# VectorE writes z in two 16-bit parts, DMAs turn them, and PSUM banks are dealt out anew

## The reference

```
q, k, v = einsum('bsd,dhk->bshk', x, W_Q / W_K / W_V)
scores  = einsum('bqhc,bshc->bhqs', q, k) / sqrt(64);  causal mask
z       = einsum('bhqs,bshc->bqhc', softmax(scores), v)
x = layernorm(x + einsum('bqhc,chd->bqd', z, W_out) + b_out)
h = layernorm(x) * gamma + beta
y = silu(h @ dequant(fc1_q, fc1_scales) + fc1_bias) @ dequant(fc2_q, fc2_scales) + fc2_bias
x = layernorm(x + (x + 0.5 * y))
```

## Time and profile before

| | |
|---|---|
| time, median of three | 2035.65 us (2034.11 to 2035.74) |
| the profiled execution's own time | 2037.36 us |
| its span, first to last instruction | 2035.4 us |
| TensorE busy | 1826.0 us, 90% |
| ScalarE busy | 1520.9 us, 75% |
| VectorE busy | 1418.6 us, 70% |
| GpSimd busy | 1319.7 us, 65% |
| DMA | 75.09 MB, mean 37 GB/s |

### The profile page before, as it was taken

One profiled execution on the slowest core, in us unless ns is written; L12 is line 12 of the kernel. 1 busy time (PEld: TensorE's weight loads), 2 busy tenths in 40 slices (PEclk: granted clock), 3 DMA queues, 4 the chain that ended last, 5 costly groups with the idle time before them and its releaser, 6 DMA issues. The chain is left out here.

```text
span 2035.4 us, 54700 instructions
## 1 busy us (share of the span) xinstructions
PE 1826.0 (90%) x22601; PEld 1299.9 (64%) x22601; DVE 1418.6 (70%) x2688; ACT 1520.9 (75%) x3151; POOL 1319.7 (65%) x738
## 2 busy tenths in 40 slices
PE   3788989999989898989899999999999977989997
PEld 2455756565656565656666666666666656878886
DVE  5886868676767676767767676768686838565663
ACT  3488887888888888888787878787879872654463
POOL 2365767686867686867676868686767786343242
PEclk8899999999999999999999999999999988999998
DMA  3002010101010101010101010101010205111210
GB/s 116 9 4 81 5 40 2 43 2 43 5 40 5 40 5 41 7 38 10 35 10 35 10 35 12 33 12 33 13 33 15 92 26 199 63 63 63 81 55 21
DMA packets 48647, 75.09 MB, mean 37 GB/s; under 512 B 5904, under 2 KB 32784, under 8 KB 48144
## 3 DMA queue, kind: packets, MB, share of 16 engines
q1 hardware_dynamic: 48400, 71.59, 11.2%
HBM read 33.82 MB, written 20.97 MB: 27 GB/s over the span
## 5 line engine op out<-in xcount | busy, mean ns | idle before, releaser
L459 POOL TENSOR_TENSOR p_lo<-p_full,p_hi 128x1024 f16<-128x1024 f32 (+1 forms) x640 | 1163.3, 1839 | 489.6 <-ACT p_full L507 489.2
L506 ACT ACTIVATE p_hi<-psum 128x512 f16<-128x512 f32 (+3 forms) x1280 | 721.7, 564 | 232.3 <-PE psum L774 123.0
L546 DVE TENSOR_REDUCE row_max<-psum 128x1 f32<-128x512 f32 (+3 forms) x1280 | 723.3, 604 | 98.3 <-PE psum L736 66.2
L507 ACT ACTIVATE p_full<-psum 128x512 f32<-128x512 f32 (+3 forms) x1280 | 729.1, 572 | 0.0
L794 PE MATMUL psum<-v,p_hi 128*128 128x65 f16 x4352 | 497.5, 193 | 36.3 <-DVE z_pair L591 34.1
L796 PE MATMUL psum<-v,p_hi 128*128 128x64 f16 x4352 | 499.9, 195 | 0.0
L798 PE MATMUL psum<-v,p_lo 128*128 128x65 f16 x4352 | 495.6, 192 | 0.0
L794 PEld LDWEIGHTS psum<-v,p_hi 128*128 128x128 f16 x4352 | 409.8, 96 | 102.5 <-issue 55.5
L768 PE MATMUL psum<-qa,ka 128*128 128x512 f16 (+3 forms) x1280 | 444.2, 348 | 24.6 <-ACT p_full L507 18.8
L772 PE MATMUL psum<-qb,kb 128*128 128x512 f16 (+3 forms) x1280 | 445.0, 348 | 0.0
L796 PEld LDWEIGHTS psum<-v,p_hi 128*128 128x128 f16 x4352 | 406.7, 97 | 55.4 <-issue 0.8
(11 more groups left out here) (126 smaller groups left out, 2991.9 us busy)
## 6 DMA issues: line engine op xcount, KB each, us to landing
zT_dram<-z_T SPq DMA_DIRECT2D x16, 1024.0 KB, 4.3
shared_z<-zT_dram SPq DMA_DIRECT2D x28, 512.0 KB, 6.3
qb<-qa SPq DMA_DIRECT2D x128, 64.0 KB, 1.9
ka<-ka SPq DMA_DIRECT2D x128, 64.0 KB, 1.9
shared_z<-xT_dram SPq DMA_DIRECT2D x8, 512.0 KB, 7.7
xs<-x_dram SPq DMA_DIRECT2D x8, 512.0 KB, 8.1
out_dram<-shared_w SPq DMA_DIRECT2D x8, 512.0 KB, 3.4
w_raw_rest<-wqkv_dram SPq DMA_DIRECT2D x1, 2304.0 KB, 14.6
```

Of the source, the lines that this page charges most:

```text
L459: nc.gpsimd.tensor_tensor(p_lo[:, at % NP, cols], p_full[:, at % NP, cols], p_hi[:, at % NP, cols], ALU.subtract).then_inc(probs_split, 1)
L506: nc.scalar.activation(p_hi[:, at % NP, to], lane_bank(a)[:, P * f:QB], ACT.Exp, scale=1.0 / SCORE)
L507: nc.scalar.activation(p_full[:, at % NP, to], lane_bank(a)[:, P * f:QB], ACT.Exp, scale=1.0 / SCORE).then_inc(lane_read, 1)
L546: nc.vector.reduce_max(row_max[:, n % MAXES, t, c:c + 1], bank_of(r)[:, 0:chunk_width(n, t, c)], AX.X).then_inc(ring_read, 1)
```

## The change

1. `outputs` writes z into `z_parts` in two float16 parts, straight from PSUM: a product for the high part, then, after a wait for it, four products with a subtraction, of 64 columns each, for the low part. `z_pair`, `turn_outputs` and `out_rows` go.
2. SP's new `out` turns a query block's parts (128 partitions x 1024 float16) with one transposing DMA into `z_T`. It waits for both heads' parts and for the store of the pair before, and SP's group copies stand behind it in SP's order. `store` of a pair moves to slot 6 of the next pair and waits for the four transposing DMAs.
3. `zT_dram` holds the two parts (as many bytes as before). `feed_forward` loads them into three buffers without splitting: `split_z` is gone on ScalarE, VectorE and GpSimd. The output projection multiplies float16 parts, and `to_norms` scales its sum by a power of two for each batch (`z_power`).
4. The output weights are loaded and split in pair 3, the fourth (`WO_UNIT`): VectorE scales and measures them at slots 6, 9, 12 and 15, `peaks` and `scales` follow at 20 and 22, ScalarE and VectorE split them at slots 26, 30, 34 and 38.
5. The ring has three banks, z two. Lanes are for scores alone.
6. `pair_order`: where a block's first products stand, ring items were put among the two scores alone; now they are spread over scores and products there too.
7. SP's last items: the load of z's block 0 (L404) stood before no wait of pair 15's outputs; now four transposing DMAs stand ahead of it.

```diff
 DVE_SHARE = 0.80
 AHEAD_BLOCKS = 2
 MAXES = 4
-Z_BANKS = 1
-RINGS = 4
+Z_BANKS = 2
+RINGS = 3
 LANES = 3
+Z_BUFS = 3
...
+    if m == WO_UNIT:
+        steps[0].append(("load_wo", m))
+        for u, i in enumerate(WO_PEAK_STEPS):
+            steps[i].append(("wo_peak", m, u))
+        steps[20].append(("peaks", m, WO_PEAK, PEAKS))
+        steps[22].append(("scales", m, WO_PEAK, PEAKS))
+        for u, i in enumerate(WO_SPLIT_STEPS):
+            steps[i].append(("wo", m, u))
+    if m:
...
-        if i - LAG in SLOT0:
-            order += step(work[:2], ring) + work[2:]
-        else:
-            order += step(work, ring) if work else ring
...
+            def out(m, q):
+
+                reach(sp, z_stored, 16 * m)
+                sp.sem_inc(passed, 1)
+                sp.wait_ge(z_done, m * NBLK + 2 * q + 2)
+                sp.sem_inc(passed, 1)
+                sp.dma_start_transpose(z_T[:, q, :, :], z_parts[:, q, :, :, :].rearrange("p a t c -> p (a t c)")
+                                       ).then_inc(z_turned[q], 16)
+
             def store(m):
 
                 if m == UNITS - 1:
-                    sp.wait_ge(x_split, B * NQ)
+                    sp.wait_ge(wo_split, PAIRS // WO_PART)
+                    sp.sem_inc(passed, 1)
                     sp.wait_ge(z_stored, 16 * PAIRS)
-                    sp.dma_start(shared[0][:, :].rearrange("p (g t) -> p g t", g=PAIRS), zT_dram[0]).then_inc(early_in, 16)
-                    sp.dma_start(shared[1][:, :].rearrange("p (g d) -> p g d", g=PAIRS), wout).then_inc(early_in, 16)
-                sp.wait_ge(lane_read, lane_place("out", m, NQ - 1) + 1)
-                sp.sem_inc(passed, 1)
+                    sp.dma_start(shared[0][:, :].bitcast(F16).rearrange("p (g t) -> p g t", g=PAIRS),
+                                 zT_dram[0].rearrange("p g a t -> p g (a t)")).then_inc(early_in, 16)
+                for q in range(NQ):
+                    sp.wait_ge(z_turned[q], 16 * m + 16)
+                    sp.sem_inc(passed, 1)
                 b, p = m // PAIRS, m % PAIRS
-                sp.dma_start(zT_dram[b * NQ:b * NQ + NQ, :, p:p + 1, :].rearrange("q p g t -> p q (g t)"),
-                             z_T[:, :, :]).then_inc(z_stored, 16)
+                sp.dma_start(zT_dram[b * NQ:b * NQ + NQ, :, p:p + 1, :, :].rearrange("q p g a t -> p q (g a t)"),
+                             z_T[:, :, :, :].rearrange("p q g t -> p q (g t)")).then_inc(z_stored, 16)
 
...
-            def out_rows(m, q):
-
-                a = lane_place("out", m, q)
-                reach(act, z_stored, 16 * m)
-                act.wait_ge(lane_ready, a + 1)
-                nc.scalar.activation(z_T[:, q, :], lane_bank(a), ACT.Copy,
-                                     scale=z_scale[:, m // PAIRS, m % PAIRS:m % PAIRS + 1]).then_inc(lane_read, 1)
+            def split_wo(u):
+
+                g = slice(WO_PART * u, WO_PART * u + WO_PART)
+                act.wait_ge(scaled, 4)
+                nc.scalar.activation(wo_parts[:, 0, g, :], wo_raw[:, g, :], ACT.Copy,
+                                     scale=scale[:, WO_PEAK:WO_PEAK + 1].bitcast(F32)).then_inc(wo_hi_done, 1)
...
-                if m:
-                    dve.wait_ge(lane_ready, lane_place("out", m - 1, q) + 1)
                 dve.wait_ge(rcp_ready, at + 1)
-                nc.vector.tensor_tensor(z_pair[:, TPB * q:TPB * q + TPB, h, :], z[:, :, 1:VZ],
-                                        z_rcp[:, at % 2, :].unsqueeze(2).to_broadcast([P, TPB, C]), ALU.mult).then_inc(z_done, 1)
+                reach(dve, z_turned[q], 16 * m)
+                z_hi, z_lo = [z_parts[:, q, a, :, C * h:C * h + C] for a in range(2)]
+                nc.vector.tensor_tensor(z_hi, z[:, :, 1:VZ], z_rcp[:, at % 2, :].unsqueeze(2).to_broadcast([P, TPB, C]),
+                                        ALU.mult).then_inc(z_hi_done, 1)
+                dve.wait_ge(z_hi_done, at + 1)
+                for t in range(TPB):
+                    last = nc.vector.scalar_tensor_tensor(out=z_lo[:, t, :], in0=z[:, t, 1:VZ], scalar=z_rcp[:, at % 2, t:t + 1],
+                                                          in1=z_hi[:, t, :], op0=ALU.mult, op1=ALU.subtract)
+                last.then_inc(z_done, 1)
...
+            def wo_peaks(m, u):
+
+                if u == 0:
+                    dve.wait_ge(wo_loaded, 16)
+                g0 = WO_PART * u
+                v_power = power[:, 1:1 + 3 * PAIRS].bitcast(F32).rearrange("p (g k) -> p g k", k=3)
+                for g in range(g0, g0 + WO_PART):
+                    nc.vector.tensor_scalar(wo_raw[:, g, :], wo_raw[:, g, :], v_power[:, g, 2:3], None, ALU.mult).then_inc(wo_scaled, 1)
+                dve.wait_ge(wo_scaled, g0 + WO_PART)
+                nc.vector.tensor_reduce(wo_peak[:, u:u + 1], wo_raw[:, g0:g0 + WO_PART, :], axis=AX.XY, op=ALU.max,
+                                        apply_absolute_value=True).then_inc(peaked, 1)
+                if u == PAIRS // WO_PART - 1:
+                    dve.wait_ge(peaked, peaks_before(("wo_peak", m, u)) + 1)
+                    nc.vector.reduce_max(peak[:, WO_PEAK:PEAKS], wo_peak[:, :], AX.X).then_inc(peaked, 1)
+
...
-            def turn_outputs(m, q):
-
-                a = lane_place("out", m, q)
-                pe.wait_ge(z_done, m * NBLK + 2 * q + 2)
-                reach(pe, lane_read, a - LANES + 1)
-                for u in range(TPB):
-                    last = nc.tensor.transpose(lane_bank(a)[:, P * u:P * u + P],
-                                               z_pair[:, TPB * q + u, :, :].rearrange("p h c -> p (h c)"), ident[:, :])
-                last.then_inc(lane_ready, 1)
...
             def load_z(i):
-                for u in range(ZQ):
-
-                    sp.wait_ge(z_split, i * ZQ - ZQ + u + 1)
+
+                if i >= Z_BUFS:
+                    sp.wait_ge(wo_ready, i - Z_BUFS + 1)
                     sp.sem_inc(passed, 1)
-                    sp.dma_start(quarter(z_raw, u), zT_dram[bass.ds(i, 1), :, GQ * u:GQ * u + GQ, :].rearrange("i p g t -> (i p) g t")
-                                 ).then_inc(z_in[u], 16)
...
-            for i in range(2):
-                for u in range(ZQ):
-                    pool.wait_ge(z_hi_done, i * ZQ + u + 1)
-                    nc.gpsimd.tensor_tensor(quarter(z_lo, u), quarter(z_raw, u), quarter(z_hi, u).bitcast(F32),
-                                            ALU.subtract).then_inc(z_split, 1)
...
+                if i:
+                    pe.wait_ge(z_in[i % Z_BUFS], 16 * (i // Z_BUFS + (i % Z_BUFS > 0)))
+                z = z_bufs[i % Z_BUFS]
                 for g in range(PAIRS):
-                    if g % GQ == 0:
-                        pe.wait_ge(z_split, i * ZQ + g // GQ + 1)
                     for t in range(TPB):
                         cols = slice(P * t, P * t + P)
-                        last = passes(psum[:, WO + t // 2, D * (t % 2):D * (t % 2) + D], (z_hi[:, g, cols], z_lo[:, g, cols]),
-                                      (wo_hi[:, g, :], wo_lo[:, g, :]), g == 0 and t % 2 == 0, g == PAIRS - 1)
-                    if g % GQ == GQ - 1:
-                        last.then_inc(wo_ready, 1)
+                        last = passes(psum[:, WO + t // 2, D * (t % 2):D * (t % 2) + D], (z[:, g, 0, cols], z[:, g, 1, cols]),
+                                      (wo_parts[:, 0, g, :], wo_parts[:, 1, g, :]), g == 0 and t % 2 == 0, g == PAIRS - 1)
+                last.then_inc(wo_ready, 1)
...
-            def split_z(i, u):
-
-                act.wait_ge(z_in[u], i * 16)
-
-                act.wait_ge(wo_ready, i * ZQ - ZQ + u + 1)
-                nc.scalar.activation(quarter(z_hi, u), quarter(z_raw, u), ACT.Copy).then_inc(z_hi_done, 1)
...
-                nc.vector.tensor_tensor(y[:, :, :], sums, xs[:, k, :, :], ALU.add).then_inc(wo_read, 1)
+                b = i // NQ
+                nc.vector.scalar_tensor_tensor(out=y[:, :, :], in0=sums, scalar=z_power[:, b:b + 1], in1=xs[:, k, :, :],
+                                               op0=ALU.mult, op1=ALU.add).then_inc(wo_read, 1)
...
-            def split_z(i):
-                for u in range(ZQ):
-                    dve.wait_ge(z_hi_done, i * ZQ + u + 1)
-                    nc.vector.tensor_tensor(quarter(z_lo, u), quarter(z_raw, u), quarter(z_hi, u).bitcast(F32),
-                                            ALU.subtract).then_inc(z_split, 1)
...
-            dve.wait_ge(early_in, 16 * 2)
-            split(Chain(wo_split, 0), wo_raw, wo_hi[:, :, :], wo_lo[:, :, :])
```

More of the change, by code:

```diff
@@ L240, in pair_order @@
     order += [("out", m, block_of(n)[1]) for n in range(1, NBLK, 2) if SLOTN[n] + LAG + 3 >= NSLOT]
-    return order + [("store", m)]
+    return order if more else order + [("store", m)]
 def first_order():
@@ L1086, in step @@
                     last.then_inc(act_ready, 1)
-                    if more == 2 and f in Z_AT:
-                        split_z(i + 2, Z_AT[f])
                     if more and f in ROOTS_AT:
```

(7 more changed lines are left out.)

124 lines of the change are left out of this document (77 added, 47 removed).

## The result

The changed kernel takes 2077.17 us (median of 4 runs, 2075.24 to 2077.74), the kernel before 2035.70 in the same session: ratio 1.0201, 95% interval 1.0184 to 1.0218. It is 2.0% slower. The forecast was 2014 us, faster by 1%, with a range up to 2060: wrong in sign and outside the range.

A forecast was written before the change was run, and what follows sets the result against it. TensorE was busy 90%, but a pair's four stretches had different limits. Attention +13, output weights +5, feed-forward -41 and between the parts +2 gave -21 us from 2035.65: 2014 us, own range 1988 to 2035, over all 1968 to 2060.

The forecast's parts named there:

- I charge two in full and the rest nothing: Attention: of eight outputs a pair, each 0.8 us longer on VectorE, only two delay the end, +1.6 us a pair.
- The comparison behind it: Pair 1's extra VectorE reductions: 4.9 us of work lengthened the pair by 3.5 us, so later ones were mostly absorbed.
- rival A: Attention: the three-bank ring's shortfalls are all paid, plus VectorE's added work in the first stretch; 2069 us, chance 0.20.
- Three ring banks: Attention: ring items wait for VectorE to release the third item before, not the fourth; +1.0 us a pair, 0 to 3.8.
- the z bank: Attention: TensorE's 2.2 us wait a pair for the single z bank brings 0 when removed, down to -2.
- the largest shortfall of the ring: Pair 9: a TensorE chunk 1.04 us late under three banks, taken to fall into TensorE's later wait for turned maxima.
- The output weights: Pair 3: four measuring steps like pair 1's reductions, +3.5 us, and four ScalarE copies, +2; taken as +5, range +2 to +10.
- TensorE's turning and ScalarE's copies: Attention: turning pieces dropped from TensorE give -0.9 us a pair, copies dropped from ScalarE -0.7.
- Feed-forward: Feed-forward blocks: without z's splitting six blocks lose 5.8 us each, -35 us, and the output projection gives -6; together -41.
- Between the parts: Attention to feed-forward: -7 us from GpSimd's splitting gone, +9 to +10 from DMAs in one queue; net +2, -5 to +8.
- SP: SP's queue: four transposing DMAs a pair delay nobody, costing 0 up to some 20 us a DMA; eight-piece estimate 10.5 us.
- rival D: SP's queue: transposing DMAs take over 20 us each and hold up group copies; some 2650 us, chance 0.04.

The follow-up runs named there:

- e5: The changed kernel without z's low-part instructions (part of the computation left out), with four ring banks and one z bank: 2014.10 us, ratio 0.9892.
- e2: The changed kernel without the four low-part instructions of each output (part of the computation left out), three ring banks and two z banks kept: 2008.85 us, ratio 0.9876.
- e9: The changed kernel with an output's four low parts placed one each behind VectorE's next four ring instructions, nothing left out: 2032.12 us, ratio 0.9971.
- e1: The changed kernel with its PSUM banks dealt as before, four ring banks and one z bank: 2129.37 us, ratio 1.0468.
- e4: The changed kernel with pair 3's eight multiplications of the output weights moved from VectorE to ScalarE: 2065.00 us, ratio 1.0148.
- e6: The changed kernel with one old order rule back, no ring work between the two products where a block's first output columns start: 2107.64 us, ratio 1.0355.

## Why the prediction was wrong

**Rows from single edits.** The steady pair, in us:

| kernel | a pair | step | forecast of the step |
|---|---|---|---|
| before | 99.2 | | |
| e5: no low parts, old banks | 99.3 | +0.1 | -0.9 - 0.7 = -1.6 |
| e2: no low parts, new banks | 98.6 | -0.7 | +1.0 |
| the change | 103.1 | +4.5 | +1.6 |

The first two forecasts, -1.6 and +1.0, stand against +0.1 and -0.7. Either two add up to -0.6: the misses cancel, by luck. The third decides.

**The step that failed** is "I charge two in full and the rest nothing". The work itself was sized well: 0.82 us an output over the kernel before and 1.43 - 0.54 = 0.89 over an output without low parts (as e9's row shows it), where 0.8 stands; that is 7.1 us a pair. But 4.5 of 7.1 us reached the end, 63%, not 1.6 of 6.4. The comparison behind it was read rightly, but was no comparison for this. Pair 1 took 3.5 us more for 4.9 us of reductions, and its clock was not looked at:

```profile
196.94:299.68 102.74, 95.93 (x1294) 63.99 (x1293) 77.75 (x150) 83.00 (x181) 72.68 (x40) 0.98 0.12 35
```

1.6 of the 3.5 come with 3.4 us at 1.2 GHz, from 272.3 on. The remaining 1.9 are 39%, and 39% of 7.1 us would have given +2.8, still short. The reductions stood by themselves, while the low parts lengthen a stretch in which VectorE already makes no maxima, at every one of the eight outputs. e9 splits the 4.5: 3.1 is the length of the stretch, 1.4 is left for the work.

The range was also narrower than its terms. The prediction's own high ends, +5.4 us a pair, +10 for the weights and +8 between the parts, add up to 2035.65 + 79 + 10 - 41 + 8 = 2092 us, and the range stopped at 2060, a part of rival A.

**Three ring banks, the z bank.** Costed apart, as +1.0 and 0. They were not separable from the length of an output: the dealing gains 0.7 us a pair with the short output and 4.4 with the long one, 2.9 at full clock (e5 and e2, e1 and the change). The prediction had the largest shortfall of the ring absorbed; the `kb` waits of 1.6 us a pair show it paid, and the z wait that went away outweighed it. Rival A had the shallow ring as its cause and gave 2069 us, near the measured 2077. Its sum is near by luck: it has 3.8 us a pair for the ring and 2.4 for VectorE's work, and the runs have -0.7 for the dealing and 4.5 for the low parts. But the place that it named is right, VectorE's added work falling where the ring runs dry. It had 0.20.

**The output weights** are the term that was mis-sized: +5 forecast, +23 over a steady pair measured. The forecast counted four reductions and four ScalarE copies and gave nothing to the eight multiplications and four low parts on VectorE: 10.9 and 5.7 us, against 2.7 and 3 at the lengths that they have when nothing meets them (340 and 743 ns). e4 shows 11.6 us of the 23 to go with the multiplications, by the price of the clock some 4.9 of them through it. Of the other 11.4 us some 3.3 are the clock's too (6.8 us at 1.2 GHz in e4), and the rest is open.

**TensorE's turning and ScalarE's copies.** Forecast -1.6 a pair; the step that holds them gave +0.1, but it also has the new order and the high part in float16, so their own worth stays open.

**Feed-forward**: -41 forecast, -43.7 from the first turning on, by the mechanism named. **Between the parts**: +2 forecast; from the last output to the first turning 44.7 us became 44.6. The part began 14.9 us after the last output (1767.16 - 1752.23) against 7.4 before, +7.5 us where +9 to +10 stood, and from there to the first turning it took 29.7 us against 37.3, -7.7 where -7 stood. **SP**: the transposing DMA landed 3.1 us after issue (median of 64, 4.8 at most) and delayed nobody seen; rival D is excluded. Eight times the 1309 ns that the Trainium skill's page "VectorE: DVE Perf Modes", section "The three transpose paths", gives for a 128x128 piece had been 10.5 us, an estimate; the trace has 3.1 for the whole DMA. The prediction's reading of the Trainium skill's same page, section "The DRAIN you can't avoid", without overlap, would give 4 x 276 = 1.10 us for the low parts; the row shows 0.86. The section itself adds that a next operation that is not held starts earlier, and with that the trace agrees: each starts 0.195 us after the one before, 0.08 before that one ends.

**The sum closes** on the profiled executions (the medians differ by 41.5 us): the attention without pair 3's excess, 82.7 - 23 = +60, where +13 stood; pair 3 +23 for +5; the rest -44 for -39. Together +39 for -21. Of the miss of 60 us, 47 lies in the steady attention, in size the low parts' 4.5 for 1.6 (2.9 us in each of 16 pairs), and 18 in pair 3, less 5 after the last output.

## What to carry to other kernels

When an engine feeds another through a few buffers, ask how long it is away at a stretch before asking how busy it is: eight outputs longer by 0.89 us in one piece cost 4.5 us a pair, in four pieces 1.4. If an unshown cost is bounded by a similar one in the trace, ask whether that one stood in the same place: here a reduction by itself was mostly absorbed, and work behind an output was not. Before two stretches are compared, compare their granted clock. Before a VectorE instruction that reads and writes SBUF is priced by its size, look whether GpSimd works at the same time.

## What was not expected of the hardware

- 3.4 us at 1.2 GHz cost a pair 1.6 us, in the kernel before (100.8 for 99.2) as in e1 (107.6 for 106.0) and e6 (106.0 for 104.4).
- VectorE, SBUF to SBUF, 128x256 float32: 340 ns free, up to 2261 ns when a GpSimd instruction of 2.13 us had started just before.
- A transposing DMA of 128x1024 float16: 1.24 us on SP's queue, 3.1 us from issue to landing.
- The low part of 64 columns out of PSUM takes 276 ns, and four of them 0.86 us: each after the first adds 0.195.
- GpSimd's float32 to float16 copy of 128x256 takes 399 ns and the subtraction 671 ns, beside 424 ns for one VectorE multiplication of that size out of PSUM.
